# DLRM tower on one core: the low parts of five tables are subtracted on POOL instead of DVE

## The chip, the cores and the metric

The kernel runs on one core of a Trainium2 chip. The metric is the device time of one execution in microseconds. Three executions of the kernel before took 543.79, 543.87 and 543.88 us, median 543.87.

## The reference

A batch of 2048 samples has one dense vector of 128 numbers and 26 embedding rows of 128 numbers each, taken from 26 tables by index. All 27 vectors of a sample are multiplied with each other, the 351 products of pairs are joined with the dense vector, and a three-layer perceptron follows.

```python
e = jnp.stack([tbl_0[ids[:, 0]], ..., tbl_25[ids[:, 25]]], axis=1)
combined = jnp.concatenate([dense_output[:, None, :], e], axis=1)
interactions = jnp.einsum('bfd,bgd->bfg', combined, combined)
z = jnp.concatenate([dense_output, interactions[:, iu, ju]], axis=1)   # pairs f < g
h = jnp.concatenate([z, dense_output], axis=1)
h = jnp.maximum(h @ W_top1 + b_top1, 0.0)      # 607 x 512
h = jnp.maximum(h @ W_top2 + b_top2, 0.0)      # 512 x 256
y = h @ W_top3                                 # 256 x 1
```

## The kernel before

The batch is worked off in eight duos of 256 samples, each in two halves of 128. Embedding rows come in two ways.

*Gathered tables* (16 of them): POOL issues one indirect DMA for each table and half (L354), 256 in all, in 64 groups of four (T0, T1, ...). A group lands in one of five slots of `E`, TensorE transposes it into a PSUM bank (`turn_gathered`, L415), ScalarE copies it to `ET`. POOL may issue group n only when group n - 5 has been transposed.

*One-hot tables* (10 small ones, eight of 1000 rows and two of 1250): these are loaded whole at the start, by SP, into places of SBUF that are free then, with 125 partitions and 8 or 10 rows of 128 numbers in each. ScalarE rounds a table to fp32r, `tab_hi` (`round_table`, L601), and the rest, `tab_lo` = raw - `tab_hi`, is subtracted by DVE (`split_table`). For the eight smaller tables ScalarE also copies the raw table into the two gram banks of PSUM (`psG`, L605), and DVE subtracts from there in two instructions of 512 columns (L741); the copy of table h waits until DVE is done with table h - 1, since the banks are the same. The two larger tables are subtracted directly in one instruction, both operands in SBUF (L736). DVE builds one-hot matrices of the ids (`build_one_hot`, L730), in a ring of four chunks; TensorE multiplies each chunk with `tab_hi` and then with `tab_lo` (`hot_chunk`, L431). A duo has 22 chunks: two for each smaller table, three for each larger one.

The order on every engine is written out by hand. `steps_of(h)` gives the list of steps of half h (0 to 16), and each engine goes through the same list and does its own part of each step. Half 0 holds the 22 chunks of duo 0 with T0 behind chunk 8, T1 behind 11, T2 behind 15 and T3 behind 18. Half 1 begins with the gram products of the first 128 samples (`gram_fill`, L457), then chunks 0 to 10 of duo 1 with T4 to T7 among them; half 2 begins with the next gram products. At the step of chunk c, DVE builds chunk c + 4, which waits until TensorE has used chunk c (`hot_used`). The split of table t stands behind the build of chunk 2t; those of the last two tables at steps 13 and 15. ScalarE rounds table t at step 2t - 4. TensorE waits for `lo_ready` before the first low-part product of a table, in duo 0 only. Gram products wait for all of `ET` of their half; ScalarE and DVE empty the two gram banks in turn.

Queues: SP loads the tables, one load of ids behind a wait for chunk 7's build, and the weights once all tables are split (`load_weights`). POOL does nothing but the gathers after its first few constants. `lo_ready` is one semaphore that counts the tables done.

Of the kernel before, what the change touches and what calls it, by code (L numbers as in the profile page):

```python
# [5 lines left out]
D = 128  # L6
# [8 lines left out]
def dlrm_program(nc, dense_pairs, dense_rows, gather_idx, hot_idx, gathered, small, W1_dense, W1_pairs,  # L15
# [187 lines left out]
    with ctx:  # L203
# [49 lines left out]
                      (raw_S, 0), (raw_S, 1), (raw_w2, 0), (raw_S[:, 2 * TABLE_K[0] * D:], 0), (raw_ET, 0)]  # L253


        VIA_PSUM = sum(k * D <= 2 * 512 for k in TABLE_K)
        REUSED = NS - 1

        def raw_table(h):
# [23 lines left out]
        zeroed, ident_ready, row_id_ready = sem("zeroed"), sem("ident_ready"), sem("row_id_ready")  # L283
        stacked_ready, U_cleared = sem("stacked_ready"), sem("U_cleared")
        row_int_ready, second_ready = sem("row_int_ready"), sem("second_ready")
        hi_ready, raw_ready, lo_ready = sem("hi_ready"), sem("raw_ready"), sem("lo_ready")
        w1d_ready, w1p_hi_ready, w1d_hi_ready = sem("w1d_ready"), sem("w1p_hi_ready"), sem("w1d_hi_ready")
        Zd_hi_ready, Zd_lo_ready = sem("Zd_hi_ready"), sem("Zd_lo_ready")
        Zp_hi_ready = sem("Zp_hi_ready")
# [20 lines left out]
        def wait_out(eng, fill):  # L310
            bank, used, _ = PLACE[fill]
            eng.wait_ge(bank_out[bank], used + 1)

        def wait_W1(eng):

# [20 lines left out]
        @block.gpsimd  # L336
        def _(pool):
            for k in K_KINDS:
                nc.gpsimd.iota(row_int[:, ROW_BASE[k]:ROW_BASE[k] + k], pattern=[[1, k]], base=0,
                               channel_multiplier=k).then_inc(row_int_ready, 1)  # L340
            nc.gpsimd.memset(ident[:, :], 0.0).then_inc(zeroed, 1)
            pool.wait_ge(zeroed, 1)
            nc.gpsimd.affine_select(out=ident[:, :], in_=ident[:, :], compare_op=ALU.not_equal,
                                    fill=1.0, base=0, pattern=[[-1, P]],
                                    channel_multiplier=1).then_inc(ident_ready, 1)
            pool.wait_ge(ident_ready, 1)
            pool.wait_ge(gidx_in[0], 16)
            for n in range(T_GROUPS):
                if n == FIRST // 4:
                    pool.wait_ge(gidx_in[1], 16)  # L350
                if n >= SLOTS:
                    wait_full(pool, ("T", n - SLOTS))
                for i in range(4):
                    nc.gpsimd.indirect_dma_start(  # L354
                        E[:, n % SLOTS, i, :], None, gathered[feature_and_tile(n, i)[0]],
                        bass.IndirectOffsetOnAxis(ap=gidx[:, 4 * n + i:4 * n + i + 1], axis=0),
                    ).then_inc(gathered_in[n % SLOTS], 16)

        @block.sync
        def _(sp):  # L360
            def load_dense(d):
                sp.dma_start(dense[:, d % 2], dense_pairs[d]).then_inc(dense_in[d % 2], 16)

            def load_table(h):
                rows = small[h].rearrange("(p k) d -> p (k d)", k=TABLE_K[h])
                if h == REUSED:
                    sp.wait_ge(raw_ready, 2)
                for part in (slice(0, SPREAD_P), slice(SPREAD_P, ROWS_P)):
                    sp.dma_start(raw_table(h)[part], rows[part]).then_inc(table_in[h], 16)

            def store_rows(d):
                wait_out(sp, ("part", d, PARTS - 1))
                sp.dma_start(out[d * DUO:(d + 1) * DUO].rearrange("(a n) o -> a (n o)", a=1),
                             Y[:, :]).then_inc(Y_out, 16)

            sp.dma_start(gidx[:, 0:FIRST], gather_idx[:, 0:FIRST]).then_inc(gidx_in[0], 16)
            load_oidx(sp, 0)
            for h in range(NS):
                load_table(h)
                if h == 2:  # L380
                    load_dense(0)
                if h in HEAD_IDS:
                    load_next_oidx(sp, HEAD_IDS[h])
            sp.dma_start(gidx[:, FIRST:], gather_idx[:, FIRST:]).then_inc(gidx_in[1], 16)
            load_dense(1)

            def load_weights():
                sp.wait_ge(lo_ready, NS)
                sp.dma_start(raw_w1p, W1_pairs.rearrange("(k p) n -> p k n", k=KP)).then_inc(w1p_in, 16)
                sp.dma_start(raw_w1d, W1_dense.rearrange("a p n -> p a n")).then_inc(w1d_in, 16)  # L390
                sp.dma_start(w2[:, :, :], W2.rearrange("(k p) n -> p k n", p=P)).then_inc(weights_in, 16)
                sp.dma_start(b1s[:, :], b1).then_inc(weights_in, 16)
                sp.dma_start(b2s[:, :], b2).then_inc(weights_in, 16)
                sp.dma_start(w3s[:, :], w3).then_inc(weights_in, 16)
                sp.dma_start(Zd[:, :], dense_rows[0]).then_inc(Zd_in, 16)

            for h in HALVES:
                for step in steps_of(h):
                    if step == ("hot", 0, FILL_LAST[HOT_FILLS + 1 - ID_RING]):
                        load_weights()  # L400
                    elif step[0] == "gram" and step[2] == G_FILLS - 1 and step[1] + 2 < DUOS:
                        sp.wait_ge(dense_out, step[1] + 1)
                        load_dense(step[1] + 2)
                    elif step[0] == "part" and step[2] == PARTS - 1:
                        store_rows(step[1])

            sp.wait_ge(Y_out, 16 * DUOS)

        @block.tensor
        def _(pe):  # L410
# [8 lines left out]
            def hot_chunk(d, c):  # L419
# [6 lines left out]
                pe.wait_ge(hot_full[m % RING], m // RING + 1)  # L426
                for tab in (tab_hi, tab_lo):
                    if d == 0 and k0 == 0 and tab is tab_lo:
                        pe.wait_ge(lo_ready, t + 1)
                    for i in range(many):  # L430
                        product = nc.tensor.matmul(  # L431
                            bank[:, t % 2 * DUO:(t % 2 + 1) * DUO], tab[0:ROWS_P, TABLE_BASE[t] + k0 + i, :],
# [165 lines left out]
        def _(act):  # L598
            def round_table(h):
                act.wait_ge(table_in[h], 32)  # L600
                nc.scalar.copy(table_rows(tab_hi, h), raw_table(h)).then_inc(hi_ready, 1)  # L601
                if h < VIA_PSUM:
                    wait_count(act, lo_ready, h)
                    for place, cols in raw_pieces(h):
                        copied = nc.scalar.copy(place, raw_table(h)[:, cols])  # L605
                    copied.then_inc(raw_ready, 1)
# [73 lines left out]
            rounded_tables = 2  # L680
            for h in HALVES:
                if h == 1:
                    act.wait_ge(lo_ready, NS)
                if h == 3:
                    act.wait_ge(weights_in, 16 * 4)
                    wait_W1(act)
# [32 lines left out]
        def _(dve):  # L719
# [13 lines left out]
            def split_table(h):  # L733
                dve.wait_ge(hi_ready, h + 1)
                if h >= VIA_PSUM:
                    nc.vector.tensor_tensor(table_rows(tab_lo, h), raw_table(h), table_rows(tab_hi, h).bitcast(f32),  # L736
                                            ALU.subtract).then_inc(lo_ready, 1)
                    return
                dve.wait_ge(raw_ready, h + 1)
                for place, cols in raw_pieces(h):  # L740
                    split = nc.vector.tensor_tensor(table_rows(tab_lo, h)[:, cols], place,  # L741
                                                    table_rows(tab_hi, h)[:, cols].bitcast(f32), ALU.subtract)
                split.then_inc(lo_ready, 1)

            def clear_G():

                dve.wait_ge(lo_ready, NS)
                for psum in psG:
                    nc.vector.memset(psum[:, :], 0.0).then_inc(G_cleared, 1)

# [52 lines left out]
            for h in HALVES:  # L803
                for step in steps_of(h):
                    if step[0] == "hot":
# [6 lines left out]
                            split_table(built_tables)  # L812
                            built_tables += 1

                        for i in range(VIA_PSUM, NS):
                            if step[1:] == (0, 2 * i - 3):
                                split_table(i)
                        if step[1:] == (0, 2 * NS - 4):
# [86 lines left out]
```

## Time and profile before

| | |
|---|---|
| median of 3 executions | 543.87 us |
| the profiled execution | 548.43 us, its span 546.6 us |
| TensorE matmul busy | 418.0 us (76%) |
| DVE busy | 275.6 us (50%) |
| POOL busy | 243.9 us (45%) |
| ScalarE busy | 142.9 us (26%) |
| mean granted clock of TensorE | 0.881 of full speed |

The times inside the profile are microseconds from the start of its span. A busy time counts an engine's instructions; waits between them are not in it. Where the profile can't name what ended a wait it says "remote", or "another core or an unknown queue".

### The profile page before, as it was taken

To read this page: it belongs to the slowest core of one execution; us is meant where nothing else is said; L and a number is where in the kernel's file an instruction comes from. 1 tells how busy PE (TensorE), PEld (TensorE's weight loads), DVE (VectorE), ACT (ScalarE), POOL (GpSimd) and SP (SyncE) were. 2 spreads that over 40 slices of the span, in tenths; PEclk is the share of its full clock that TensorE was granted. 3 is DMA by queue.
4 is the path that set the end of the run, shared out by engine and by line. 5 is a ranking of instruction groups with operands and counts; after the bars stand their busy time and mean duration, and the time that the engine had idled before them with its cause. 6 is when DMAs were issued, how large, how long until landed. Compare 5 with 4: busy or idle time off the path is not lost.

```text
span 546.6 us, 10182 instructions
## 1 busy us (share of the span) xinstructions
PE 418.0 (76%) x4392; PEld 385.7 (71%) x4392; DVE 275.6 (50%) x365; ACT 142.9 (26%) x355; POOL 243.9 (45%) x264
## 2 busy tenths in 40 slices
PE   2477765759878596985969768794887949778998
PEld 2466664759776595975959768693886849767987
DVE  4389853854445454444454545445552465434322
ACT  4355121522122111222112222122221222112432
POOL 6726373553626355262553616446163552616100
PEclk9869995978889798787988879799787989979999
DMA  7954631221212112121221211222020311211000
GB/s 201 259 141 105 200 85 33 83 62 38 66 42 79 49 49 69 40 74 44 54 62 50 72 36 58 58 65 71 27 86 28 83 43 38 80 31 38 22 11 1
DMA packets 19775, 37.38 MB, mean 68 GB/s; under 512 B 5930, under 2 KB 8626, under 8 KB 19732
## 3 DMA queue, kind: packets, MB, share of 16 engines
q0 software_dynamic: 8192, 16.79, 11.5%
q1 hardware_dynamic: 5492, 9.85, 6.8%
q10 hardware_dynamic: 6048, 10.10, 6.0%
q8 instruction: 35, 0.57, 0.4%
q14 instruction: 8, 0.07, 0.0%
HBM read 36.71 MB, written 0.01 MB: 67 GB/s over the span
## 4 chain that ended last, share of the span: by engine, by line
PE 56%; another core or an unknown queue 19%; issue 10%; ACT 7%; DVE 5%; DMA 2%; SPq 1%; DVEq 0%; ACTq 0%
PE psB L431 19%; PE psG L457 14%; PE psB L506 7%; PE psB L415 6%; PE psB L513 6%; PE psB L500 3%; DVE one_hot L730 3%; ACT ET L633 2%; DMA ET<-tbl 2%; ACT ET L653 2%; PE psB L468 1%; DVE tab_lo L741 1%; ACT Zp L672 1%; ACT psG L605 1%
## 5 line engine op out<-in xcount | busy, mean ns | idle before, releaser
L354 POOL DMA_INDIRECT E<-tbl,gidx x256 | 243.0, 949 | 264.2 <-PE psB L415 163.5
L730 DVE TENSOR_TENSOR one_hot<-oidx,psR 125x1024 fp32r<-125x1024 int32 (+1 forms) x176 | 200.8, 1169 | 172.0 <-remote 130.7
L431 PE MATMUL psB<-one_hot,tab_hi 125*128 125x256 f32 x672 | 126.1, 308 | 24.4 <-issue 11.7
L457 PE MATMUL psG<-ET 128*52 128x52 f32 x2048 | 87.5, 259 | 70.8 <-issue 38.7
L457 PEld LDWEIGHTS psG<-ET 128*52 128x52 f32 x2048 | 79.2, 172 | 79.5 <-issue 45.6
L431 PE MATMUL psB<-one_hot,tab_lo 125*128 125x256 f32 x672 | 118.7, 296 | 14.4 <-issue 11.3
L431 PEld LDWEIGHTS psB<-one_hot,tab_hi 125*128 125x128 f32 x672 | 99.4, 202 | 31.7 <-issue 26.5
L431 PEld LDWEIGHTS psB<-one_hot,tab_lo 125*128 125x128 f32 x672 | 99.0, 201 | 16.7 <-issue 12.7
L633 ACT COPY ET<-psB 128x512 f32<-128x512 f32 x64 | 40.8, 638 | 89.2 <-PE psB L415 58.1
L777 DVE COPY_PREDICATED S<-second,psG 116x208 f32<-116x208 int32 x64 | 25.0, 391 | 50.1 <-ACT S L662 49.6
L662 ACT COPY S<-psG 116x208 f32<-116x208 f32 x64 | 21.3, 332 | 100.8 <-PE psG L457 95.3
L653 ACT COPY ET<-psB 128x256 f32<-128x256 f32 x80 | 27.5, 404 | 75.2 <-remote 46.4
L415 PE MATMUL psB<-ident,E 128*128 128x128 f32 x256 | 41.4, 287 | 0.9 <-issue 0.9
L506 PE MATMUL psB<-Zp,w1p_hi 128*128 128x256 f32 x192 | 38.9, 299 | 0.0
L415 PEld LDWEIGHTS psB<-ident,E 128*128 128x128 f32 x256 | 31.7, 149 | 1.7 <-issue 1.1
L506 PEld LDWEIGHTS psB<-Zp,w1p_hi 128*128 128x128 f32 x192 | 32.4, 207 | 0.1
L513 PE MATMUL psB<-ZH,w 128*128 128x256 f32 x128 | 32.0, 395 | 0.0
L506 PE MATMUL psB<-Zp,w1p_lo 128*128 128x256 f32 x96 | 28.7, 299 | 0.0
L513 PEld LDWEIGHTS psB<-ZH,w 128*128 128x128 f32 x128 | 24.1, 198 | 3.3
L468 PE MATMUL psB<-ident,S 116*128 116x116 f32 x104 | 15.5, 272 | 12.5 <-issue 7.8
L468 PEld LDWEIGHTS psB<-ident,S 116*128 116x128 f32 x104 | 11.2, 141 | 16.4 <-issue 10.7
L592 ACT ACTIVATE ZH<-psB,b1s 128x256 f32<-128x256 f32 x16 | 7.6, 475 | 56.9 <-remote 43.3
(55 smaller groups left out, 217.3 us busy)
## 6 DMA issues: line engine op xcount, KB each, us to landing
oidx<-hot_idx ACTq DMA_DIRECT2D x35, 256.0 KB
E<-tbl,gidx POOLq DMA_INDIRECT x256
ET<-tbl SPq DMA_DIRECT2D x3, 448.0 KB
oidx<-hot_idx SPq DMA_DIRECT2D x5, 256.0 KB
dense<-dense_pairs SPq DMA_DIRECT2D x8, 128.0 KB
ZH<-tbl SPq DMA_DIRECT2D x2, 448.0 KB
S<-tbl SPq DMA_DIRECT2D x2, 448.0 KB
Zd<-dense_rows ACTq DMA_DIRECT2D x7, 128.0 KB, 2.0
```

The lines of the kernel that those rows point to most:

```text
L354: nc.gpsimd.indirect_dma_start(E[:, n % SLOTS, i, :], None, gathered[feature_and_tile(n, i)[0]], bass.IndirectOffsetOnAxis(ap=gidx[:, 4 * ...
L415: turned = nc.tensor.transpose(bank[:, i * P:(i + 1) * P], E[:, n % SLOTS, i, :], ident[:, :])
L431: product = nc.tensor.matmul(bank[:, t % 2 * DUO:(t % 2 + 1) * DUO], tab[0:ROWS_P, TABLE_BASE[t] + k0 + i, :], one_hot[0:ROWS_P, m % RING, ...
L457: gram = nc.tensor.matmul(psG[g % 2][q * LANE:q * LANE + M, a * M:(a + 1) * M], two[:, 0:M], two[:, PAIR:], start=True, stop=True)
L468: turned = nc.tensor.transpose(bank[:, i * P:i * P + MT], two, ident[0:MT, 0:MT])
L506: layer = nc.tensor.matmul(bank[:, 0:DUO], w[:, kp, cols], z[:, kp, :], start=False, stop=(kp == KP - 1 and w is w1p_lo))
L513: layer = nc.tensor.matmul(bank[:, 0:DUO], w2[:, q, cols], h1[:, q, :], start=(q == 0), stop=(q == M1 - 1))
L633: copied = nc.scalar.copy(features(tile, 1 + feature_and_tile(n, i)[0], many), bank[:, i * P:(i + many) * P].rearrange("p (f j h s) -> p f ...
L653: copied = nc.scalar.copy(features(2 * d + half, 1 + NG + first, many), psB[bank][:, 0:many * DUO].rearrange("p (f t j h s) -> p t f j h s ...
L662: nc.scalar.copy(gram_rows(d, i), gram_samples(g, 0)).then_inc(G_first[g % 2], 1)
L730: nc.vector.tensor_tensor(one_hot[0:ROWS_P, m % RING, 0:many], ids, rows, ALU.is_equal).then_inc(hot_full[m % RING], 1)
L777: nc.vector.copy_predicated(gram_rows(d, i), mine, gram_samples(g, 1)).then_inc(G_out[g % 2], 1)
```

## The change

Tables 0, 1 and 2 are split as before, by way of PSUM. Table 3 is now subtracted by POOL behind its gathers of group 3, tables 4 to 7 behind those of group 4, each in one instruction of 125x1024 with both operands in SBUF, after a wait for the table's rounded part. Tables 8 and 9 stay on DVE, directly. ScalarE no longer copies tables 3 to 7 into PSUM. Since two engines now finish tables, `lo_ready` becomes ten semaphores, one for each table; who waited for all ten counts now waits for each of the ten, and the clear of the gram banks waits for tables 0 to 2 alone.

```diff
--- before.py
+++ after.py
@@ -253,7 +253,10 @@
                       (raw_S, 0), (raw_S, 1), (raw_w2, 0), (raw_S[:, 2 * TABLE_K[0] * D:], 0), (raw_ET, 0)]
 
 
-        VIA_PSUM = sum(k * D <= 2 * 512 for k in TABLE_K)
+
+        VIA_PSUM = 3
+        POOL_SPLITS = {3: (3,), 4: (4, 5, 6, 7)}
+        DIRECT = (8, 9)
         REUSED = NS - 1
 
         def raw_table(h):
@@ -283,7 +286,7 @@
         zeroed, ident_ready, row_id_ready = sem("zeroed"), sem("ident_ready"), sem("row_id_ready")
         stacked_ready, U_cleared = sem("stacked_ready"), sem("U_cleared")
         row_int_ready, second_ready = sem("row_int_ready"), sem("second_ready")
-        hi_ready, raw_ready, lo_ready = sem("hi_ready"), sem("raw_ready"), sem("lo_ready")
+        hi_ready, raw_ready, lo_ready = sem("hi_ready"), sem("raw_ready"), sems("lo_ready", NS)
         w1d_ready, w1p_hi_ready, w1d_hi_ready = sem("w1d_ready"), sem("w1p_hi_ready"), sem("w1d_hi_ready")
         Zd_hi_ready, Zd_lo_ready = sem("Zd_hi_ready"), sem("Zd_lo_ready")
         Zp_hi_ready = sem("Zp_hi_ready")
@@ -310,6 +313,10 @@
         def wait_out(eng, fill):
             bank, used, _ = PLACE[fill]
             eng.wait_ge(bank_out[bank], used + 1)
+
+        def wait_tables(eng):
+            for low in lo_ready:
+                eng.wait_ge(low, 1)
 
         def wait_W1(eng):
 
@@ -355,6 +362,10 @@
                         E[:, n % SLOTS, i, :], None, gathered[feature_and_tile(n, i)[0]],
                         bass.IndirectOffsetOnAxis(ap=gidx[:, 4 * n + i:4 * n + i + 1], axis=0),
                     ).then_inc(gathered_in[n % SLOTS], 16)
+                for h in POOL_SPLITS.get(n, ()):
+                    pool.wait_ge(hi_ready, h + 1)
+                    nc.gpsimd.tensor_tensor(table_rows(tab_lo, h), raw_table(h),
+                                            table_rows(tab_hi, h).bitcast(f32), ALU.subtract).then_inc(lo_ready[h], 1)
 
         @block.sync
         def _(sp):
@@ -385,7 +396,7 @@
             load_dense(1)
 
             def load_weights():
-                sp.wait_ge(lo_ready, NS)
+                wait_tables(sp)
                 sp.dma_start(raw_w1p, W1_pairs.rearrange("(k p) n -> p k n", k=KP)).then_inc(w1p_in, 16)
                 sp.dma_start(raw_w1d, W1_dense.rearrange("a p n -> p a n")).then_inc(w1d_in, 16)
                 sp.dma_start(w2[:, :, :], W2.rearrange("(k p) n -> p k n", p=P)).then_inc(weights_in, 16)
@@ -426,7 +437,7 @@
                 pe.wait_ge(hot_full[m % RING], m // RING + 1)
                 for tab in (tab_hi, tab_lo):
                     if d == 0 and k0 == 0 and tab is tab_lo:
-                        pe.wait_ge(lo_ready, t + 1)
+                        pe.wait_ge(lo_ready[t], 1)
                     for i in range(many):
                         product = nc.tensor.matmul(
                             bank[:, t % 2 * DUO:(t % 2 + 1) * DUO], tab[0:ROWS_P, TABLE_BASE[t] + k0 + i, :],
@@ -600,7 +611,8 @@
                 act.wait_ge(table_in[h], 32)
                 nc.scalar.copy(table_rows(tab_hi, h), raw_table(h)).then_inc(hi_ready, 1)
                 if h < VIA_PSUM:
-                    wait_count(act, lo_ready, h)
+                    if h:
+                        act.wait_ge(lo_ready[h - 1], 1)
                     for place, cols in raw_pieces(h):
                         copied = nc.scalar.copy(place, raw_table(h)[:, cols])
                     copied.then_inc(raw_ready, 1)
@@ -680,7 +692,7 @@
             rounded_tables = 2
             for h in HALVES:
                 if h == 1:
-                    act.wait_ge(lo_ready, NS)
+                    wait_tables(act)
                 if h == 3:
                     act.wait_ge(weights_in, 16 * 4)
                     wait_W1(act)
@@ -734,17 +746,18 @@
                 dve.wait_ge(hi_ready, h + 1)
                 if h >= VIA_PSUM:
                     nc.vector.tensor_tensor(table_rows(tab_lo, h), raw_table(h), table_rows(tab_hi, h).bitcast(f32),
-                                            ALU.subtract).then_inc(lo_ready, 1)
+                                            ALU.subtract).then_inc(lo_ready[h], 1)
                     return
                 dve.wait_ge(raw_ready, h + 1)
                 for place, cols in raw_pieces(h):
                     split = nc.vector.tensor_tensor(table_rows(tab_lo, h)[:, cols], place,
                                                     table_rows(tab_hi, h)[:, cols].bitcast(f32), ALU.subtract)
-                split.then_inc(lo_ready, 1)
+                split.then_inc(lo_ready[h], 1)
 
             def clear_G():
 
-                dve.wait_ge(lo_ready, NS)
+                for h in range(VIA_PSUM):
+                    dve.wait_ge(lo_ready[h], 1)
                 for psum in psG:
                     nc.vector.memset(psum[:, :], 0.0).then_inc(G_cleared, 1)
 
@@ -812,7 +825,7 @@
                             split_table(built_tables)
                             built_tables += 1
 
-                        for i in range(VIA_PSUM, NS):
+                        for i in DIRECT:
                             if step[1:] == (0, 2 * i - 3):
                                 split_table(i)
                         if step[1:] == (0, 2 * NS - 4):
```

## Rows read from the trace of the kernel before

**Rows 1.** The page, the chain that ended last: share of the span by engine.

```profile
PE 56%; another core or an unknown queue 19%; issue 10%; ACT 7%; DVE 5%; DMA 2%; SPq 1%; DVEq 0%; ACTq 0%
```

**Rows 2.** The page, costliest groups: busy us, mean ns | idle before, releaser.

```profile
L354 POOL DMA_INDIRECT E<-tbl,gidx x256 | 243.0, 949 | 264.2 <-PE psB L415 163.5
L730 DVE TENSOR_TENSOR one_hot<-oidx,psR 125x1024 fp32r<-125x1024 int32 (+1 forms) x176 | 200.8, 1169 | 172.0 <-remote 130.7
```

**Rows 3.** Timeline of POOL, 0 to 70: start us, us, instruction [idle before <-releaser].

```profile
1.36 0.29 POOL L343 TENSOR_SCALAR_AFFINE_SELECT ident<-ident 128x128 f32<-128x128 f32 x1 [0.16 <-POOL ident L341]
...
22.16 0.94 POOL L354 DMA_INDIRECT E<-tbl,gidx  x1 [0.30 <-issue]
...
27.15 0.94 POOL L354 DMA_INDIRECT E<-tbl,gidx  x1 [0.30 <-issue]
37.81 0.94 POOL L354 DMA_INDIRECT E<-tbl,gidx  x1 [9.72 <-PE psB L415]
...
49.80 0.94 POOL L354 DMA_INDIRECT E<-tbl,gidx  x1 [2.31 <-PE psB L415]
51.04 1.45 POOL L354 DMA_INDIRECT E<-tbl,gidx  x1 [0.30 <-issue]
...
59.94 0.94 POOL L354 DMA_INDIRECT E<-tbl,gidx  x1 [0.30 <-issue]
68.59 0.94 POOL L354 DMA_INDIRECT E<-tbl,gidx  x1 [7.71 <-PE psB L415]
```

**Rows 4.** Timeline of DVE, 14 to 62.

```profile
28.74 1.22 DVE L730 TENSOR_TENSOR one_hot<-oidx,psR 125x1024 fp32r<-125x1024 int32 x1 [9.93 <-remote]
...
34.31 1.29 DVE L741 TENSOR_TENSOR tab_lo<-psG,tab_hi 125x512 fp32r<-125x512 f32 x2 [0.36 <-ACT psG L605]
35.52 2.34 DVE L730 TENSOR_TENSOR one_hot<-oidx,psR 125x1024 fp32r<-125x1024 int32 x2
37.78 1.28 DVE L741 TENSOR_TENSOR tab_lo<-psG,tab_hi 125x512 fp32r<-125x512 f32 x2
...
44.69 1.28 DVE L741 TENSOR_TENSOR tab_lo<-psG,tab_hi 125x512 fp32r<-125x512 f32 x2
...
50.19 1.48 DVE L736 TENSOR_TENSOR tab_lo<-S,tab_hi 125x1280 fp32r<-125x1280 f32 x1
```

**Rows 5.** Timeline of ScalarE, 14 to 50.

```profile
17.55 1.05 ACT L601 CAST tab_hi<-ZH 125x1024 fp32r<-125x1024 f32 x1 [1.26 <-issue]
...
31.60 0.69 ACT L653 COPY ET<-psB 128x256 f32<-128x256 f32 x2 [11.99 <-remote]
32.15 1.06 ACT L601 CAST tab_hi<-ZH 125x1024 fp32r<-125x1024 f32 x1
...
41.08 1.04 ACT L601 CAST tab_hi<-w 125x1024 fp32r<-125x1024 f32 x1
```

**Rows 6.** Timeline of TensorE's matmuls, 14 to 32 and 70 to 90.

```profile
15.13 1.09 PE L431 MATMUL psB<-one_hot,tab_lo 125*128 125x256 f32 x4
...
76.62 0.91 PE L431 MATMUL psB<-one_hot,tab_lo 125*128 125x256 f32 x4
86.64 2.67 PE L457 MATMUL psG<-ET 128*52 128x52 f32 x56 [9.11 <-issue]
```

**Rows 7.** Timeline of POOL: last gathers of three later runs without a gap.

```profile
82.32 0.94 POOL L354 DMA_INDIRECT E<-tbl,gidx  x1 [0.30 <-issue]
...
151.34 0.94 POOL L354 DMA_INDIRECT E<-tbl,gidx  x1 [0.30 <-issue]
...
182.91 0.94 POOL L354 DMA_INDIRECT E<-tbl,gidx  x1 [0.30 <-issue]
```

**Rows 8.** Stretches, L457 alone: from:to, us, busy (count), clock, DMA, GB/s.

```profile
60.30:64.90 4.60, 3.71 (x128) 3.31 (x128) 1.00 0.93 317
...
148.30:157.80 9.50, 5.82 (x128) 5.02 (x128) 0.82 0.11 30
186.30:191.80 5.50, 5.22 (x128) 5.10 (x128) 0.59 0.17 51
```

**Rows 9.** The chain that ended last, 60 to 160: start us, us, what.

```profile
154.08 3.67 PE psG L457 x96
```

## The prediction

> **What bounds the kernel now.** I read the page's chain of waits first: TensorE holds 56% of it, and the second entry, 19%, is no engine but "another core or an unknown queue" [rows 1]. There is one core, so that entry has to be something else. The costliest groups say who meets it: the one-hot builds on DVE spend most of their idle time, 130.7 us, on "remote", and POOL's gathers spend 163.5 us waiting for a transpose to free a slot [rows 2]. So over the whole run neither DVE nor POOL is short of time; they wait for TensorE, and something besides the matmuls themselves makes its signals late.
>
> Then I read the first 62 us engine by engine, because all that the change touches lies there. POOL issues five groups of four gathers back to back, each gather 1.25 us after the last, the 16th at 22.16 and the 20th ending at 28.09. It is idle until 37.81, when the first slot is free, gathers groups 5 and 6, waits 2.31 us, and gathers groups 7 and 8 until 60.88 [rows 3]. DVE has an idle stretch of 9.93 us ending at 28.74, though the chunk whose buffer it wants had been multiplied by 16.2; ScalarE has one of 11.99 us ending at 31.60 [rows 4 to 6]. After that DVE is the pacemaker of the head: one split through PSUM (1.29) and two builds (2.34) a table, hardly any gap, splits starting at 34.31, 37.78, and so on to 44.69 [rows 4].
>
> The late signals have a pattern. A run of gathers ends at 83.26 and the stopped TensorE goes on at 86.64, after 9.11 us of nothing, its last matmul before that being at 77.5 [rows 6, 7]. A run of gathers ends at 152.28, and the gram products, which crawl from 148.3, run freely only from 154.08; 128 of them take 9.5 us there and 5.5 us where the last gather (183.85) was over before they began [rows 7 to 9]. In the first 60 us: the last of 20 gathers ends at 28.09, the stalls end at 28.74 and 31.60. So while POOL gathers and TensorE is busy, TensorE's releases arrive late, and they come in a lump within 1 to 3.5 us of the last gather. That is a reading of rows, not a mechanism that I know, but it decides this case: what a run of gathers ends at matters more than how busy POOL is. The profiled execution took 548.43 against a median of 543.87, so nearly all of what these rows show is there without the profiler too.
>
> **The change part by part.** *Removed from DVE:* ten subtractions of 512 columns, five tables at 1.28 us = 6.4 us, inside the stretch where DVE sets the pace. *Removed from ScalarE:* ten copies to PSUM, about 1.1 us a table, 5.5 us, and with them its waits for DVE's previous split. ScalarE isn't the pacemaker there, so this only brings its casts forward. *Added to POOL:* five subtractions of 125x1024 with two SBUF inputs. No row shows one. The nearest is POOL's affine_select, 0.29 us for 128 columns [rows 3]: eight times that is 2.3 us, which charges its fixed part eight times too, so it can stand for the second input; twice that, 4.6, is the upper bound. The lower is DVE's own direct split, 1.48 us for 1280 columns [rows 4], so 1.2 for 1024. I take 2.3. *Semaphores:* one counter becomes ten; waits on counters long reached cost nothing that a row shows. The clear of the gram banks waits for three tables instead of ten; it came after the last split anyway, at 56 us, and in DVE's own order it still does.
>
> The Trainium skill ("GPSIMD Engine Reference", Performance versus the Vector engine) speaks against such a move: it gives 4497 ns on GpSimd and 2293 ns on VectorE for a two-input fp32 op of 2048 columns. Half of that is an estimate of 2.25 us by that page, and with it the sum below would be 0.2 us lower. No row here shows either.
>
> Now POOL's queue, in order. (a) Table 3 is split behind group 3, which ends at 23.10. Its rounded part was ready at 18.60 [rows 5], so there is no wait, and group 4 is 2.3 us late: it ends at 30.4 and not at 28.09. It is wanted by TensorE at 68, so that itself costs nothing. (b) Tables 4 to 7 come before group 5. Table 4's rounded part ended at 33.21, since ScalarE stood until 31.60 [rows 5]; I leave that time as it is. From 33.2, four splits of 2.3 end at 42.4. Table 7's rounded part is there in time: its cast started at 41.08, but behind copies to PSUM that waited for DVE; without them it ends at about 40, and the fourth split begins at 40.1. (c) Groups 5 to 8 stand behind all this. Before, they took from 37.81 to 60.88, 23.1 us, of which 2.0 was the wait for the third slot beyond the usual gap; now that slot is free in time. 42.7 + 21.1 = 63.8. So POOL's idle 9.7 us takes up most of the 11.5 us, yet not all, because it can't start on table 4 before 33.2.
>
> For the data itself 63.8 would do: group 5 is not wanted before 70. DVE gets the head done earlier: table 7's low part is there at 42.4 and not at 45.97, and with no splits of tables 3 to 7 the next two builds are already made, so that table 8's split ends at about 45.4 and not at 51.67, 6.3 us earlier. Taken alone the head would give that. But the gram products of the first half then start at about 54 inside a run of gathers that lasts until 63.8, where before they began at 60.3 as the run ended (60.88) and were through at 64.8 [rows 3, 8]. With the run as the gate the gram products end at 63.8 + 3.9 = 67.7 and not 64.8: **2.9 us later**. What follows keeps this: the next run of gathers starts when TensorE turns the next group (68.59), TensorE stops at 77.5 and waits for that run's end, so there is no slack to win it back. The sum is 548.43 + 2.9 = 551.3 for a profiled execution, and 543.87 + 2.9 = **546.8** for the median.
>
> One contention I looked for: a gather took 1.45 us instead of 0.94 at 51.04, beside DVE's direct split of 50.19 to 51.67 [rows 3, 4]. DVE's builds of one-hots run beside dozens of gathers that stay at 0.94. A build reads one operand from SBUF and one from PSUM, the direct splits read two from SBUF; so I expect POOL's new splits, too, to run undisturbed by builds, and the two direct splits to meet gathers as before. Were builds to hold up the splits, four waits of up to 1.2 us would put the sum at 551.6.
>
> **The rivals.** *R1, the head's gain stays:* the gathers don't gate the first gram products. For it: these very products were the ones least disturbed before, and signals were prompt in the run that began at 49.80. Against: of the stretches in [rows 8], the one inside a run takes 9.5 us. Up to 6.3 us earlier: 537.6, or 541 if half of it survives. *R2, the gram products are held fully:* they lie deep inside the run, as at 148, and end 5.5 us after its last gather (157.8 - 152.28) and not 3.9: 1.6 more, 548.4; and if the signals of the last chunks are held as well, up to 3 us beyond. *R3, it fits the gap:* the pause behind group 3 lets TensorE's held signals out early, ScalarE rounds table 4 by 30.7, the four splits end at 39.9 and the run at 61.3, 0.4 later than before: no change, 544.3. It is also what comes out if 28.74 and 31.60 are due to the table loads and not to the gathers. *R4, POOL's price is the upper one:* four times 2.3 more, 556.0; at the lower one, table 7's cast at 40 is the limit, its split ends at 41.2, the run at 62.6: +1.7, 545.6, inside the forecast's range.
>
> **How the numbers follow.** Forecast 0.34, R1 0.35, R2 0.13, R3 0.15, R4 0.03. The forecast and R1 are nearly level; I forecast slower since R2 and R4 go the same way. A measurement of this kernel can tell about 0.2%, 1.1 us, from no change. Faster by more than that: 0.35. Within it: 0.15. Slower: 0.50. The likeliest case alone spans 545.5 to 548.5; with R1 and R2 the range is 539.0 to 551.5.
>
> **What would show it.** Right: POOL subtractions of about 2.3 us, the last ending near 42.4; a run of 16 gathers without a gap ending near 64; DVE's split of table 8 ending near 45 although the first gram products end near 68. Wrong: gram products that run at full rate inside that run (R1), the first stalls of DVE and ScalarE ending near 24 instead of 29 to 32 (R3), or subtractions of another length.

## The result: slower by 0.4 to 0.6%, with two errors in the working that cancelled

Timed against the kernel before on one chip, the changed kernel took 546.68 us (median of 5 executions, 544.85 to 547.89) where the kernel before took 543.79: ratio 1.0058, interval 1.0032 to 1.0085, so 3.2 us more. Timed again later (e5 below) the ratio was 1.0043 (1.0021 to 1.0065), 2.3 us more. 546.8 had been forecast.

Chips differ here by more than the change does: the kernel before takes 543 to 544 us on one chip and 548 to 549 on another. The profile of 548.43 shown ahead of the prediction is of the second sort and that of the changed kernel (546.68) of the first, so those two can't be subtracted over their whole length, and the 551.3 forecast for a profiled execution has nothing to be held against. The 4.6 us between 548.43 and 543.87 aren't the profiler's: in e1 the profiled execution took 548.6 and the others of the same kernel 547.2 to 553.0. In what follows totals are compared by the ratios of runs that shared a chip, and later stretches by e5 and e6, the two kernels profiled on the same chip.

### The profile page after: what moved, and what is told of

Its sections match the earlier page's. It is cut to its first block, busy times and chain, and to the rows that moved or that the text cites. A ratio compares the mean times of both kernels' runs of the same rounds, so it can differ in the third digit from the quotient of the medians.

```text
span 544.9 us, 10172 instructions
## 1 busy us (share of the span) xinstructions
PE 419.3 (77%) x4392; PEld 391.3 (72%) x4392; DVE 270.7 (50%) x355; ACT 138.1 (25%) x345; POOL 255.6 (47%) x269
## 3 DMA queue, kind: packets, MB, share of 16 engines
q0 software_dynamic: 8192, 16.79, 12.5%
## 4 chain that ended last, share of the span: by engine, by line
PE 63%; another core or an unknown queue 15%; issue 11%; POOL 4%; ACT 4%; DVE 3%; DMA 0%; DVEq 0%; ACTq 0%; POOLq 0%
PE psB L442 22%; PE psG L468 16%; PE psB L517 7%; PE psB L426 6%; PE psB L524 5%; POOL E L361 3%; PE psB L511 2%; PE psB L529 2%; DVE one_hot L742 1%; ACT ET L645 1%; PE psB L479 1%; ACT ET L665 1%; POOL tab_lo L367 1%; ACT Zp L684 1%
## 5 line engine op out<-in xcount | busy, mean ns | idle before, releaser
L468 PE MATMUL psG<-ET 128*52 128x52 f32 x2048 | 91.3, 264 | 77.6 <-issue 46.1
L468 PEld LDWEIGHTS psG<-ET 128*52 128x52 f32 x2048 | 82.7, 177 | 86.9 <-issue 54.0
L442 PE MATMUL psB<-one_hot,tab_hi 125*128 125x256 f32 x672 | 128.7, 313 | 20.0 <-ACT tab_hi L612 9.8
L442 PE MATMUL psB<-one_hot,tab_lo 125*128 125x256 f32 x672 | 117.5, 296 | 7.9 <-issue 5.7
L442 PEld LDWEIGHTS psB<-one_hot,tab_hi 125*128 125x128 f32 x672 | 102.2, 207 | 27.0 <-issue 24.3
L426 PE MATMUL psB<-ident,E 128*128 128x128 f32 x256 | 43.1, 296 | 0.6 <-DVE w1d_lo L777 0.6
L426 PEld LDWEIGHTS psB<-ident,E 128*128 128x128 f32 x256 | 33.0, 153 | 1.2 <-issue 0.8
L524 PE MATMUL psB<-ZH,w 128*128 128x256 f32 x128 | 30.7, 384 | 0.0
L603 ACT ACTIVATE ZH<-psB,b1s 128x256 f32<-128x256 f32 x16 | 7.6, 475 | 56.5 <-remote 42.5
```

Of the source, the lines that this page charges most:

```text
L426: turned = nc.tensor.transpose(bank[:, i * P:(i + 1) * P], E[:, n % SLOTS, i, :], ident[:, :])
L442: product = nc.tensor.matmul(bank[:, t % 2 * DUO:(t % 2 + 1) * DUO], tab[0:ROWS_P, TABLE_BASE[t] + k0 + i, :], one_hot[0:ROWS_P, m % RING, ...
L468: gram = nc.tensor.matmul(psG[g % 2][q * LANE:q * LANE + M, a * M:(a + 1) * M], two[:, 0:M], two[:, PAIR:], start=True, stop=True)
L524: layer = nc.tensor.matmul(bank[:, 0:DUO], w2[:, q, cols], h1[:, q, :], start=(q == 0), stop=(q == M1 - 1))
```

## Time and profile after

Timeline of POOL in the changed kernel, as in [rows 3]: start, duration, instruction, and in brackets the idle time before it.

```profile
22.28 0.95 POOL L361 DMA_INDIRECT E<-tbl,gidx  x1 [0.30 <-issue]
23.25 2.35 POOL L367 TENSOR_TENSOR tab_lo<-ZH,tab_hi 125x1024 fp32r<-125x1024 f32 x1
25.76 0.96 POOL L361 DMA_INDIRECT E<-tbl,gidx  x1 [0.16 <-issue]
...
29.52 0.94 POOL L361 DMA_INDIRECT E<-tbl,gidx  x1 [0.30 <-issue]
30.49 2.35 POOL L367 TENSOR_TENSOR tab_lo<-ZH,tab_hi 125x1024 fp32r<-125x1024 f32 x1
32.80 4.72 POOL L367 TENSOR_TENSOR tab_lo<-S,tab_hi 125x1024 fp32r<-125x1024 f32 x2
37.50 2.37 POOL L367 TENSOR_TENSOR tab_lo<-w,tab_hi 125x1024 fp32r<-125x1024 f32 x1
40.03 0.96 POOL L361 DMA_INDIRECT E<-tbl,gidx  x1 [0.16 <-issue]
...
43.79 1.19 POOL L361 DMA_INDIRECT E<-tbl,gidx  x1 [0.30 <-issue]
...
46.53 1.84 POOL L361 DMA_INDIRECT E<-tbl,gidx  x1 [0.30 <-issue]
...
59.90 0.94 POOL L361 DMA_INDIRECT E<-tbl,gidx  x1 [0.30 <-issue]
70.27 0.94 POOL L361 DMA_INDIRECT E<-tbl,gidx  x1 [9.42 <-PE psB L426]
```

The five splits are there, 2.35 to 2.40 us each, and the idle stretch of 9.7 us is gone. The four stand back to back from 30.49: none waited for its table. The run of 16 gathers that follows has no gap and ends at 60.84, practically where it ended before (60.88).

Timeline of DVE and then of ScalarE, as in [rows 4] and [rows 5]:

```profile
24.42 1.22 DVE L742 TENSOR_TENSOR one_hot<-oidx,psR 125x1024 fp32r<-125x1024 int32 x1 [5.04 <-remote]
...
42.67 1.49 DVE L748 TENSOR_TENSOR tab_lo<-S,tab_hi 125x1280 fp32r<-125x1280 f32 x1
...
46.07 1.49 DVE L748 TENSOR_TENSOR tab_lo<-ET,tab_hi 125x1280 fp32r<-125x1280 f32 x1
```

```profile
18.16 1.05 ACT L612 CAST tab_hi<-ZH 125x1024 fp32r<-125x1024 f32 x1 [1.29 <-DMA ZH<-tbl]
26.57 0.68 ACT L665 COPY ET<-psB 128x256 f32<-128x256 f32 x2 [7.36 <-remote]
27.13 1.04 ACT L612 CAST tab_hi<-ZH 125x1024 fp32r<-125x1024 f32 x1
```

DVE is done with table 8 at 44.16, 7.5 us earlier than at 51.67. The two stalls end at 24.42 and 26.57, where [rows 4, 5] have 28.74 and 31.60: the first inside the pause that the split of table 3 makes in the gathers (23.2 to 25.8), the second 0.8 us behind it. And this is where all of it goes, TensorE's matmuls of the first gram products:

```profile
51.30 0.63 PE L442 MATMUL psB<-one_hot,tab_lo 125*128 125x256 f32 x4
55.23 1.50 PE L468 MATMUL psG<-ET 128*52 128x52 f32 x33 [3.29 <-issue]
57.26 0.43 PE L468 MATMUL psG<-ET 128*52 128x52 f32 x3 [0.54 <-issue]
59.39 0.34 PE L468 MATMUL psG<-ET 128*52 128x52 f32 x2 [1.70 <-issue]
60.12 0.24 PE L468 MATMUL psG<-ET 128*52 128x52 f32 x1 [0.38 <-issue]
61.52 0.43 PE L468 MATMUL psG<-ET 128*52 128x52 f32 x3 [1.16 <-issue]
62.92 3.57 PE L468 MATMUL psG<-ET 128*52 128x52 f32 x86 [0.97 <-issue]
```

A quarter of them run, then they come one to three at a time while POOL gathers, and the rest runs without a stop from 62.92, 2.1 us after the last gather. They end at 66.5; before it was 64.8.

The clock has a part in this. TensorE does nothing from 51.9 to 55.2 and little until 62.9; its granted clock goes from 1.00 to 0.50 between 55 and 56 and is back at 1.00 only at 66. The last matmuls of these products, columns as in [rows 8], in the changed kernel and then in the kernel before:

```profile
62.90:66.50 3.60, 3.57 (x86) 3.40 (x85) 0.61 0.00 0
```

```profile
63.00:64.90 1.90, 1.75 (x64) 1.63 (x64) 1.00 0.68 248
```

At the second pace the 86 would take 2.4 us and not 3.6: an estimate of 1.2 us for the clock, in the part behind the last gather alone.

## The experiments

In the diffs `wait_full(pool, ("T", n - SLOTS))` is POOL's wait for a free slot; `G_out[1]` counts emptied fills of the second gram bank.

**e1: the kernel before, again.**

> The kernel before once more, unchanged, for a second profile of it: the first profiled execution took 548.43 us where the others took 542.7 to 543.9. Theory G (a run of gathers that passes through gram products holds them) needs the first gram products to end near 64.8 us again. Rival C (the later halves differ from one execution to the next by TensorE's clock and its waits, and that is all there is) expects head milestones to move by over 1 us between two profiles of the same kernel, and a span other than 546.6.

548.50 us, ratio 0.9996 (0.9976 to 1.0015). Its first gram products end at 65.2, its run of gathers at 60.9, its span is 546.8. So the first profile was an ordinary one of this chip, and the two ends, of the run and of the products, repeat within 0.4 us. C's expectation of over 1 us fails for these, but not for DVE's first stall, which ends at 30.23 here and at 28.74 in the first profile.

**e2: group 8 held back.**

```diff
                 if n >= SLOTS:
                     wait_full(pool, ("T", n - SLOTS))
+                if n == 8:
+                    pool.wait_ge(G_out[1], 2)
```

> The changed kernel, but POOL gathers group 8 only once the first half's gram products have been emptied. Theory G: the run of gathers from 40.0 ends after 12 gathers at about 56, not at 60.9; the first gram products are free from about 57.5 and end near 61.5 (66.6 in the changed kernel, 64.8 before), and about 5 us of it stay: 541.5 us. Rival C: the head ends earlier but the total stays within 1 us of the changed kernel's 546.7. Rival P (POOL's subtractions take something from DVE or TensorE through SBUF): nothing changes, 546.7.

549.34 us, ratio 1.0012 (0.9991 to 1.0032) to the kernel before. G's 541.5 would be 0.996 and P's 546.7 would be 1.005; both fail. C's figure, 1.0035 or more, is only just above the interval. The head did what G said: the last gather before the gram products starts at 55.10, and they end at 61.7, 4.8 us earlier than in the changed kernel. The same products of two neighbouring halves, and the last gather of the next run:

```profile
52.40:61.80 9.40, 7.27 (x128) 6.14 (x128) 0.50 0.45 149
83.70:96.20 12.50, 7.10 (x128) 5.86 (x128) 0.63 0.14 36
```

```profile
89.47 0.94 POOL L363 DMA_INDIRECT E<-tbl,gidx  x1 [0.30 <-issue]
```

The gain of 3.5 us against e1 is gone 34 us later: the next gram products begin at 83.8 instead of 87.0, but now a run of eight gathers (80.71 to 90.41) goes through them, where before it was four, and they end at 96.1, as in e1 (95.9). G had named the gate for one half only and had not asked which run stands at the next.

**e3: DVE subtracts directly, POOL gathers alone.**

```diff
-        VIA_PSUM = sum(k * D <= 2 * 512 for k in TABLE_K)
+        VIA_PSUM = 3
...
-                            if step[1:] == (0, 2 * i - 3):
+                            if step[1:] == (0, 2 * i - (3 if i >= NS - 2 else 4)):
```

> The kernel before, with tables 3 to 7 subtracted by DVE directly from SBUF, one instruction a table, and no copy to PSUM: ScalarE is relieved, POOL does gathers alone. Theory G: DVE's pace per table stays near 3.5 us (1.2 and two builds of 1.2), the gathers run as before; 543.8 us within 1. Rival P: DVE with two operands in SBUF meets the gathers of groups 5 and 6 (37.8 to 47.5), gathers of 1.4 to 1.8 us, the run about 2 us later: 545 or more.

549.83 us, ratio 1.0025 (1.0010 to 1.0040): 1.4 us slower than before, past G's bound and what P had (545 or more, 1.002). P's gathers are there too. Three of POOL's and two of DVE's rows:

```profile
37.81 1.52 POOL L354 DMA_INDIRECT E<-tbl,gidx  x1 [9.69 <-PE psB L415]
...
40.88 1.85 POOL L354 DMA_INDIRECT E<-tbl,gidx  x1 [0.31 <-issue]
...
44.28 1.84 POOL L354 DMA_INDIRECT E<-tbl,gidx  x1 [0.30 <-issue]
```

```profile
37.29 1.22 DVE L736 TENSOR_TENSOR tab_lo<-S,tab_hi 125x1024 fp32r<-125x1024 f32 x1
...
40.69 1.22 DVE L736 TENSOR_TENSOR tab_lo<-S,tab_hi 125x1024 fp32r<-125x1024 f32 x1
```

Three gathers beside the new direct splits take 1.52, 1.85 and 1.84 us where others take 0.94, 2.4 us more together. That the run ends only 0.4 us later than before, at 61.3, comes of the other thing that moved: chunks came a little earlier, so the third slot was free in time and the 2.0 us of waiting for it are gone. The gram products began at 58.2 inside the run, went through it and ended at 66.6.

```profile
58.00:66.70 8.70, 6.92 (x128) 6.28 (x128) 0.50 0.57 192
```

**e4: POOL works for nothing, DVE as before.**

```diff
+                for h in {3: (3,), 4: (4, 5, 6, 7)}.get(n, ()):
+                    pool.wait_ge(hi_ready, h + 1)
+                    if h > 3:
+                        pool.wait_ge(idle_work, h - 3)
+                    nc.gpsimd.tensor_tensor(<w1p_lo>, <tab_hi of table 0>, <tab_hi of table 1>, ALU.subtract).then_inc(idle_work, 1)
```

> The kernel before with all its splits on DVE, and in addition five subtractions of 125x1024 by POOL where the changed kernel has them, from other operands into a buffer not in use yet; they serve nothing. Theory G: POOL starts them at 33.2 (tables' rounded parts wait for DVE as before, the last at 42.1), the last ends near 45, the run of 16 gathers near 66, the first gram products near 71: 5 to 6 us slower than before, 549. Rival P: the same POOL work costs what the changed kernel lost, 3 us, wherever the run ends. Rival C: within 1 us of before.

552.81 us, ratio 1.0063 (1.0041 to 1.0085), 2.2 to 4.7 us; between two profiles of one chip, span 552.1 against e1's 546.8, 5.3 us. The diff is cut: operands in angle brackets are named by what they are, and DVE waits for all five subtractions before it writes to their buffer. G's 5 to 6 us for the total are above the interval, and the ratio alone would fit rival P as well; the place fits G: the run ends at 64.5, 3.6 later than in e1, the gram products at 70.1, 4.9 later, and that carries through to the end.

```profile
60.20:70.20 10.00, 6.60 (x128) 5.68 (x128) 0.55 0.30 89
```

**e5 and e6: both kernels on one chip.**

> The changed kernel once more, unchanged, on the same chip as the kernel before and its profile. Theory G: head as in its first profile (run of 16 gathers ending near 60.8, first gram products ending near 66.5), and the 1.7 us by which it is behind there still there at the end: 1.5 to 3 us slower than before. Rival C (the rest of the kernel wanders by more than that from chip to chip): the head is 1.7 us behind but the total is within 1 us of before.

> The kernel before, for its profile on this chip. Theory G: gram products of the first half end at 64.8 to 65.2, and each later group of gram products is behind in the changed kernel by 1 to 4 us. Rival C: from about 250 us on the two are in either order.

e5 took 546.64 us, ratio 1.0043 (1.0021 to 1.0065); e6, one execution, 543.3. The gram products of the first, second, seventh and last half, first in the kernel before (e6), then in the changed one (e5); columns as in [rows 8]:

```profile
59.90:64.70 4.80, 3.76 (x128) 3.42 (x128) 1.00 0.92 317
86.20:95.20 9.00, 6.80 (x128) 6.07 (x128) 0.51 0.11 31
250.50:256.20 5.70, 5.44 (x128) 5.32 (x128) 0.56 0.16 49
520.60:524.40 3.80, 3.52 (x128) 3.26 (x128) 1.00 0.01 4
```

```profile
52.40:67.50 15.10, 8.28 (x128) 7.14 (x128) 0.50 0.37 120
89.30:98.30 9.00, 7.02 (x128) 5.99 (x128) 0.50 0.12 31
254.10:259.70 5.60, 5.43 (x128) 5.30 (x128) 0.56 0.14 50
524.30:528.10 3.80, 3.52 (x128) 3.26 (x128) 1.00 0.02 4
```

7.5 us ahead at the first start, 2.8 behind at its end, then 3.1, 3.5 and 3.7 behind: made in one place and kept for 460 us. Rival C falls. In that place the clock column differs as well, 1.00 and 0.50, and the same 128 matmuls are 3.76 us busy and 8.28. In e5 the run of 16 gathers ends a little later than in the first profile, at 61.5, and the gram products at 67.4.

**e7 and e8: the last group, or the last two, held back in every half.**

```diff
+                if n > 4 and n % 4 == 0:                      # e7
+                    pool.wait_ge(G_out[1], 2 * ((n - 4) // 4))
...
+                if n > 4 and n % 4 in (0, 3):                 # e8
+                    pool.wait_ge(G_out[1], 2 * ((n - 3) // 4 if n % 4 == 3 else (n - 4) // 4))
```

> The changed kernel, with POOL holding back in every half the group that would be gathered during the gram products (groups 8, 12, 16, ...) until these are emptied. Theory G: gram products of the halves with an even number, 8.5 to 10.5 us while a run passes through them, take 5 to 6; some 4 us in each of seven halves, 20 us or more of it kept: 525. Rival K (the late signals are conserved: what gathers don't hold in the gram products they hold later, in the chunks): total within 3 us of the changed kernel.

> As the one before, but the last two groups of each half are held back (7, 8, 11, 12, ...). Theory G: no gather in any group of gram products; the same 20 us or more, perhaps less since group 4h + 7 is wanted at the end of the half in which it is then gathered. Rival K: runs of 16 gathers after the gram products, TensorE's signals late in the chunks for longer, 546 or more.

e7: **520.85 us**, ratio 0.9544 (0.9496 to 0.9591), 25 us faster than before. e8: 583.69 us, ratio 1.0718 (1.0682 to 1.0754), 39 us slower. G had 525 for the first and the same for the second. Rival K had no change for the first and a loss for the second. Each is right once. Gram products of four halves in e7:

```profile
56.40:62.40 6.00, 5.79 (x128) 5.66 (x128) 0.50 0.18 57
82.80:90.50 7.70, 6.05 (x128) 5.48 (x128) 0.55 0.20 56
110.00:120.20 10.20, 6.34 (x128) 5.81 (x128) 0.68 0.19 55
207.70:211.60 3.90, 3.51 (x128) 3.25 (x128) 1.00 0.02 4
```

Some are now undisturbed (3.9 us where e6 takes 10), some not: runs of gathers from 81.1 to 85.8 and from 104.3 to 114.1 reach into the second and the third. The first has no gather in it and still takes 6.0, at a clock of 0.50, where the last one shown takes 3.9 at 1.00. In e8 none has a gather, and each group of gram products takes 3.6 to 5.4 us. But every run after them is one of 16 gathers, and TensorE stands still inside it, waiting for banks that ScalarE or DVE have not emptied, since TensorE's signal that they are full came late. POOL's, ScalarE's and TensorE's rows:

```profile
90.43 0.94 POOL L363 DMA_INDIRECT E<-tbl,gidx  x1 [11.78 <-issue]
...
109.20 0.95 POOL L363 DMA_INDIRECT E<-tbl,gidx  x1 [0.31 <-issue]
```

```profile
107.47 0.36 ACT L573 COPY ZH<-psB 128x8 f32<-128x8 f32 x3 [6.51 <-remote]
```

```profile
101.01 0.84 PE L481 MATMUL psB<-ident,S 116*128 116x116 f32 x3 [1.98 <-issue]
107.89 0.65 PE L481 MATMUL psB<-ident,S 116*128 116x116 f32 x2 [6.03 <-issue]
...
114.37 1.09 PE L495 MATMUL psB<-ident,ZH 128*128 128x128 f32 x4 [4.53 <-ACT ZH L573]
```

ScalarE waits until 107.47 for a bank that TensorE had filled by 96.6, and TensorE goes on at 107.89 as soon as the bank is empty. Gathered data are not what it waits for: the next group that it turns had been issued from 90.43 to 95.1. So it isn't gram products alone that a run holds: whatever hands work back and forth between TensorE and its emptiers is held. The waits "remote" of DVE's builds are 193.8 us in all in e8, 118.9 in e7, 107.2 in e6; since e7 has more of them than e6 and is faster, the sum says little, and the place of a wait counts. Part of e8's loss is the clock. Two groups of four transposes, before and behind a standstill of 6.4 us:

```profile
243.34 0.59 PE L481 MATMUL psB<-ident,S 116*128 116x116 f32 x4 [1.36 <-issue]
250.33 1.04 PE L481 MATMUL psB<-ident,S 116*128 116x116 f32 x4 [6.40 <-issue]
```

The granted clock is 1.00 until 246 and 0.50 from 248 to 256, and over the whole run its mean is 0.824, where e6 has 0.887; TensorE's matmuls are busy for 424.8 us against 409.2, which is 15.6 of the 39 us. That a run of 16 costs more than two of 8 is an inference from this one kernel: e8 differs from e7 in the length of the runs and in where they stand.

**e9 to e12.** e9 is e7's hold in the kernel before. e10 holds in the changed kernel only groups 8, 12, 16 and then every second one. e11 splits tables 3 and 4 on POOL and 5 to 7 directly on DVE, with no hold. e12 is the kernel before.

```diff
-                if n > 4 and n % 4 == 0:
+                if n > 4 and n % 4 == 0 and (n <= 16 or n % 8 == 4):   # e10
...
-        POOL_SPLITS = {3: (3,), 4: (4, 5, 6, 7)}
-        DIRECT = (8, 9)
+        POOL_SPLITS = {3: (3,), 4: (4,)}                                 # e11
+        DIRECT = (5, 6, 7, 8, 9)
```

> The kernel before (splits all on DVE, gathers alone on POOL) with the last group of each half held back until the gram products are emptied, the same hold as in the run of 520.9. Theory G: the first gram products gain little, since their run ended with them; the later ones gain as much as in the changed kernel: 520 to 524. If the hold only repairs what POOL's splits did, it stays near 544.

> The changed kernel, with groups 8, 12 and 16 held back and after that only the last groups before gram products of halves with an even number, since in the kernel before no run passed through the others. Theory G: as with all held, 521 within 3; faster if a hold before the other halves costs something by itself. Rival K (the gain comes from shorter runs everywhere, not from the gram products): slower than 521 by 5 or more.

> Only tables 3 and 4 are split on POOL, tables 5 to 7 by DVE directly from SBUF, no hold. Theory G: POOL is free at 32.8, groups 5 to 8 begin when the first slot is free, near 36, and end at 57 to 58; the first gram products then end at 62 to 64: 0 to 2 us faster than before, where the full change is 2.4 slower. Rival P (POOL's subtractions as such cost): slower than before by two fifths of 2.4, 1 us.

> The kernel before, for its profile on the chip of these runs: gram products as in the other profiles of it, the first ending near 64.8, those of the halves with an even number taking 9 to 10.5 us.

e9: 531.91 us, ratio 0.9695 (0.9667 to 0.9722). The hold is worth 3% without POOL's splits, so it doesn't just repair them; with them it is worth more (0.9544), which the forecast of 520 to 524 had missed. Its first gram products end at 65.9, e7's at 62.3, so 3.6 of the difference is the head; the rest lies in how later runs fall and is not explained. e10: 524.82 us, ratio 0.9578 (0.9543 to 0.9613): not told apart from e7, as G had it; K's 526 or more (0.967 against 544.05) falls. e11: 546.27 us, ratio 0.9956 (0.9938 to 0.9975): **2.4 us faster** than before, where the full change is 2.3 to 3.2 slower. POOL is free at 32.9, the run goes from 35.8 to 58.7 (0.7 later than forecast: four gathers beside direct splits took 1.47 to 1.85), and the products end at 63.7 (65.6 in e12):

```profile
55.50:63.80 8.30, 5.36 (x128) 4.66 (x128) 0.85 0.58 198
```

The same subtraction on the same engine makes the kernel faster with two tables and slower with five; rival P falls. The nearer partner is e3, where DVE does all the splits directly: it was 1.4 us slower than before. e12 is near what was expected, its first gram products ending at 65.6 and not at 64.8, 0.4 later than in e1.

## Why the prediction was right

The direction was right for the reason given. The size, 2.9 us against 3.2 and 2.3 measured, was luck in part: two terms were off by 2 to 3 us each and cancelled.

*The gate.* Last gather before the end of the first gram products, start and end of these products, the distance from the first to the last of the three, and the granted clock over the products, in all fourteen profiles:

| | last gather ends | products start | end | distance | clock |
|---|---|---|---|---|---|
| before | 60.9 | 60.3 | 64.8 | 3.9 | 1.00 |
| e6 (before) | 60.6 | 60.0 | 64.6 | 3.9 | 1.00 |
| e12 (before) | 61.7 | 60.6 | 65.6 | 3.8 | 1.00 |
| e1 (before) | 60.9 | 60.3 | 65.2 | 4.2 | 0.67 |
| e11 | 58.7 | 55.6 | 63.7 | 5.1 | 0.85 |
| e3 | 61.3 | 58.2 | 66.6 | 5.3 | 0.50 |
| e10 | 57.1 | 53.6 | 62.6 | 5.5 | 0.50 |
| e4 | 64.5 | 60.3 | 70.1 | 5.6 | 0.55 |
| e2 | 56.1 | 52.5 | 61.7 | 5.6 | 0.50 |
| changed | 60.8 | 55.2 | 66.5 | 5.7 | 0.55 |
| e5 (changed) | 61.5 | 52.5 | 67.4 | 5.9 | 0.50 |
| e7 | 55.9 | 56.5 | 62.3 | 6.5 | 0.50 |
| e8 | 50.9 | 52.4 | 57.4 | 6.5 | 0.62 |
| e9 | 54.9 | 61.4 | 65.9 | 11.1 | 1.00 |

Where a run goes through the products, their start says nothing on their end (the changed kernel starts 2.7 us later than e5 and ends 0.9 earlier) and the end of the run does. e7, with the same head as e2, starts its products only behind the run, 4.0 later than e2, and ends them 0.7 later. That is the step that carried the forecast, and it is shown by the two runs that change POOL's queue alone: e2 ends the run 4.8 us earlier than the changed kernel and the products 4.8 us earlier; e4 ends the run 3.6 us later than e1 and the products 4.9 us later. e8 and e9 show the other gate. With the last gather over well before the products, they end 4.6 to 5.0 us after their own start: 57.4 in e8, so DVE's earlier head is worth 7.2 us against e6 once no gather is in the way, which R1 had priced at 6.3. In the kernel before it was this gate that counted and not the run: e9 takes the last four gathers away, and the products still end at 65.9.

*POOL's price:* 2.3 taken, 2.35 to 2.40 measured, next to DVE's builds and without one being longer. The estimate by the Trainium skill ("GPSIMD Engine Reference", Performance versus the Vector engine), half its figure for 2048 columns, was 2.25; the trace is 0.1 above that. *DVE's relief:* 6.3 us earlier forecast for the end of table 8's split, 7.5 measured, and as forecast none of it survives.

*The start of the four splits was wrong.* I left table 4's rounded part at 33.2; it was there at 28.17 and the splits began at 30.49, as R3 had it. ScalarE's stall ends at 31.5 to 31.7 in the six profiles without a pause behind group 3 (before, e1, e3, e6, e9, e12) and at 26.5 to 29.1 in the eight with one, so the pause does let that signal out. It is not due to the table loads, R3's other reading: the DMA engines are fully busy when the stall ends at 26.57. That put the end of the run at 60.8 to 61.5 and not at 63.8. *The distance from the run's end was wrong too:* 3.9 taken from before, 5.7 to 5.9 measured, near R2's 5.5. The 3.9 was no distance from a gate; it was the time of the products themselves, which began as the run ended and ran at a clock of 1.00. [rows 8] shows the clock of each stretch (1.00, 0.82, 0.59), and I put what it costs at nothing. The sum came out as 2.9 because 2.3 to 3.0 us too much in one term met 1.8 to 2.0 too little in the other; at the end of the products 1.7 us are measured in the first profile and 2.8 between e5 and e6. The case that happened is R3's start with R2's hold; I had priced them apart and never together, and 61.3 + 5.5 was to be had from my own numbers: 66.8, 2.0 late.

*That it stays:* right for a loss. The distance at the first half grows by 0.9 us only until the last (e5, e6), and e4's 4.9 is 5.4 at the end. A gain stays in e11 (1.9 us at the first products and at the last) and does not in e2, where the next run then stood in the next products.

*The contention:* the two gathers beside DVE's direct splits took 1.19 and 1.84 us, where two had taken 1.45 [rows 3] and 1.84 before; e3 has five of them. The Trainium skill ("SBUF — State Buffer", Who interferes with whom) has a rule for that: a DVE instruction with two SBUF inputs contends with a GpSimd instruction that reads SBUF. The traces agree if a gather is taken for such an instruction; the same section infers the contrary for descriptor generation, and here the measured 1.19 to 1.85 us against 0.94 decide. Builds, with one input in SBUF, left POOL's two-input splits at 2.35 to 2.40.

*What stays open.* Why TensorE's signals are late while POOL gathers is not known, nor whether issuing the gathers or the moving of their data does it; no run parts the two. POOL's arithmetic doesn't: from 31.8 to 39.9 in the changed kernel, while POOL subtracts, DVE and ScalarE have no wait "remote". Nor do the DMA engines as such: e9's products take 4.6 us with the engines 74% busy and no gather. The signals don't always wait for a run's end either, as the lump of the prediction would have it. The kernel before in e6, where POOL gathers without a pause until 28.2:

```profile
23.06 1.22 DVE L730 TENSOR_TENSOR one_hot<-oidx,psR 125x1024 fp32r<-125x1024 int32 x1 [4.66 <-remote]
```

This is the stall that ends at 28.74 in [rows 4] and at 30.23 in e1. Only TensorE's signals are late: DVE's wait in [rows 4] was for a chunk multiplied 12 us before, and no wait on ScalarE's or DVE's signals of that kind was found. That it is not made by the profiler is shown by e7 and e8, whose times of 521 and 584 us are those of plain executions.

## What to carry to other kernels

Filling an engine's idle time moves what stands behind it in its queue; ask where the end of that work will fall, not whether it is still in time for its reader. Here the work was gathers, and a run of them through a stretch that passes banks between engines is what costs, twice over where the standstill takes TensorE's clock to 0.50. Where a profile shows long waits by nobody ("remote", an unknown queue) in a program on one core, line their ends up with the ends of other engines' runs before pricing anything: the best version (e7, 4.6% faster than before, with the five splits on POOL and one more wait) came from that reading and not from the change.

## What the runs showed of the hardware that was not expected

A matmul's release reached DVE 12.5 us after the matmul (16.2 to 28.74) while 20 gathers were issued back to back beside loads of tables. A pause of 2.5 us in them, from 23.2 to 25.8, let out a release that ScalarE otherwise gets at 31.5 to 31.7, at 26.57. DVE's own first release is less regular: 23.06 to 30.23 in four profiles of the kernel before.

The place of the gathers is worth 12% of the kernel's time. With all gathers of a half in one run of 16 it is 7% slower, with runs of 4, 8 and 12 that mostly stand off the gram products 4.6% faster, at the same work and the same bytes. Matmuls are busy for 409.2 us in e6 and 412.9 in e7, so that gain is all in waits; in e8 they are busy for 424.8, at a mean clock of 0.824.

The same 128 small matmuls without a gather in them take 3.6 us at a granted clock of 1.00 (e8, 226.0 to 229.7) and 5.8 at 0.50 (e7, 56.5 to 62.3), behind a standstill of 4.6 us.
